# Two of the probability chunks of a tile turned by DMA instead of by TensorE

## What is computed

```
xn = layernorm(x)
scores = (xn @ W_qk) @ xn^T / 16 + (kpos - qpos) * slope, causal
s = softmax(scores) @ (xn @ W_v^T)
g = silu(top-1 mixture of 8 experts (256 -> 1024 -> 256) of xn, 512 tokens for each expert at most)
out = x + s * g
```

## Time and profile before

| | us |
|---|---|
| median of 3 runs | 500.19 (499.97 to 501.13) |
| profiled execution | 500.93 |
| its span | 499.2 |
| PE busy | 443.4 (89%) |
| DVE busy | 352.4 (71%) |
| ACT busy | 258.1 (52%) |
| POOL busy | 229.4 (46%) |

### The profile page before, as it was taken

One profiled execution on the slowest core, in us unless ns is written; L12 is line 12 of the kernel. 1 busy time (PEld: TensorE's weight loads), 2 busy tenths in 40 slices (PEclk: granted clock), 3 DMA queues, 4 the chain that ended last, 5 costly groups with the idle time before them and its releaser, 6 DMA issues.

```text
span 499.2 us, 8775 instructions
## 1 busy us (share of the span) xinstructions
PE 443.4 (89%) x3137; PEld 303.3 (61%) x3137; DVE 352.4 (71%) x949; ACT 258.1 (52%) x540; POOL 229.4 (46%) x339
## 2 busy tenths in 40 slices
PE   2778498989999898998999999999999999999970
PEld 1345265666677775675776678666666666666650
DVE  2869478688676777787776564597888979787440
ACT  1443334445455533453533445686776868677640
POOL 4218641460514072645013000328787687878761
PEclk9979789999999998999999999999999999999995
DMA  8961430430710186406001504408577574752140
GB/s 265 372 258 44 129 127 19 128 120 6 208 44 0 23 282 189 145 2 191 21 1 37 130 13 169 128 9 247 177 204 222 158 234 116 244 128 74 62 126 31
DMA packets 64315, 63.45 MB, mean 127 GB/s; under 512 B 36902, under 2 KB 58156, under 8 KB 62224
## 3 DMA queue, kind: packets, MB, share of 16 engines
q1 hardware_dynamic: 53472, 40.78, 27.9%
q0 software_dynamic: 5632, 16.73, 10.5%
q10 hardware_dynamic: 5168, 5.37, 3.3%
HBM read 30.29 MB, written 25.43 MB: 112 GB/s over the span
## 4 chain that ended last, share of the span: by engine, by line
PE 36%; DVE 32%; ACT 11%; issue 5%; POOL 5%; SPq 1%; DMA 1%; POOLq 0%; DVEq 0%; ACTq 0%
PE bank L1101 11%; PE bank L1103 11%; PE bank L1102 11%; DVE pmax L825 7%; DVE w_l L851 6%; DVE hid_l L869 4%; PE bank L1172 4%; ACT sc L1004 4%; DVE sc L794 3%; DVE pT_l L807 2%; POOL xn L518 2%; ACT hid_h L1027 2%; ACT hid L1025 1%; ACT w_h L1016 1%; POOL slots L572 1%
## 5 line engine op out<-in xcount | busy, mean ns | idle before, releaser
L1010 ACT ACTIVATE pT_h<-bank 128x512 f16<-128x512 f32 (+2 forms) x80 | 42.0, 528 | 75.2 <-PE bank L1172 75.1
L807 DVE TENSOR_TENSOR pT_l<-bank,pT_h 128x512 f16<-128x512 f32 (+2 forms) x80 | 48.5, 607 | 37.1 <-ACT pT_h L1010 37.1
L1101 PE MATMUL bank<-v_h,pT_h 128*128 128x256 f16 x272 | 74.2, 273 | 0.4 <-DVE pT_l L807 0.4
L1102 PE MATMUL bank<-v_l,pT_h 128*128 128x256 f16 x272 | 74.2, 273 | 0.0
L1103 PE MATMUL bank<-v_h,pT_l 128*128 128x256 f16 x272 | 74.2, 273 | 0.0
L1004 ACT ACTIVATE sc<-sc,nbias 128x512 f32<-128x512 f32 (+2 forms) x80 | 51.8, 649 | 43.1 <-DVE nbias L800 43.1
L1101 PE MATMUL bank<-w_h,hid_h 128*128 128x256 f16 x256 | 69.9, 273 | 2.9 <-DVE w_l L851 2.8
L869 DVE TENSOR_TENSOR hid_l<-hid,hid_h 128x512 f16<-128x512 f32 x64 | 50.1, 789 | 29.7 <-ACT hid_h L1027 29.6
L1102 PE MATMUL bank<-w_l,hid_h 128*128 128x256 f16 x256 | 69.8, 273 | 0.0
L1103 PE MATMUL bank<-w_h,hid_l 128*128 128x256 f16 x256 | 69.8, 273 | 0.0
L1101 PE MATMUL bank<-xT,qT_h 128*128 128x512 f16 (+3 forms) x160 | 56.1, 354 | 8.2 <-DVE cmax L794 5.7
(11 more groups left out here) (164 smaller groups left out, 986.4 us busy)
## 6 DMA issues: line engine op xcount, KB each, us to landing
raw<-in_w_e SPq DMA_DIRECT2D x5, 2048.0 KB, 8.8
sc<-in_w_e SPq DMA_DIRECT2D x3, 2048.0 KB, 7.6
slots<-empty ACTq DMA_DIRECT2D x1, 4224.0 KB, 28.9
out<-xg SPq DMA_DIRECT2D x8, 512.0 KB, 3.3
rows<-xg SPq DMA_DIRECT2D x8, 512.0 KB, 4.4
rows<-so SPq DMA_DIRECT2D x8, 512.0 KB, 3.0
xg<-in_x SPq DMA_DIRECT2D x6, 512.0 KB, 4.3
xg<-in_x ACTq DMA_DIRECT2D x2, 512.0 KB, 6.0
```

What stands on the lines that cost most here:

```text
L807: v.tensor_tensor(pT_l[:, t % 2, cols], tr_ps[n % 2][:, 0:w], pT_h[:, t % 2, cols], ALU.subtract).then_inc(pT_lo, 1)
L1010: a_.activation(pT_h[:, t % 2, c * GTOK:c * GTOK + w], tr_ps[n % 2][:, 0:w], ACT.Copy).then_inc(pT_hi, 1)
L1101: pe.matmul(ps, a_h, b_h, start=first, stop=False, skip_group_check=shared)
L1102: pe.matmul(ps, a_h, b_l, start=False, stop=False, skip_group_check=shared)
```

## The change

In tiles with three or four chunks, chunks 0 and 2 no longer go through PE's turn. ACT copies the probabilities to f16 directly behind their exponential, in query layout, into a slot of `hid_h`; DVE makes the low half into `hid_l` at the head of step 0 or 1 (`low_early`), ahead of the score it reads there; and SP issues two DMA transposes for the chunk (`turn_p`), into `pT_h` and `pT_l`. Both chunks of tile t stand in SP's list ahead of what it had for tile t. PE's `values` wait for the two landings. The other chunks keep their way, with the two banks counted by `turn_no`.

```diff
+def by_dma(t, c):
+    return chunks(t) >= 3 and c % 2 == 0
+def dma_no(t, c):
+    return sum(by_dma(k, q) for k in range(t) for q in range(chunks(k))) + sum(by_dma(t, q) for q in range(c))
+def turn_no(t, c):
+    return chunk_no(t, c) - dma_no(t, c)
...
 SP
+            def turn_p(t, c):
+                d, w = dma_no(t, c), chunk_blocks(t, c) * P
+                cols = slice(c * GTOK, c * GTOK + w)
+                sp.wait_ge(p_lo, d + 1)
+                sp.wait_ge(pv_full, t - 1)
+                for half, turned_half in ((hid_h, pT_h), (hid_l, pT_l)):
+                    sp.dma_start_transpose(turned_half[:, t % 2, cols].rearrange("p (q n) -> p q n", n=P),
+                                           half[:, d % HB, 0:w]).then_inc(pT_in[d % HB], 16)
...
             for t in range(TILES):
                 g = t // GT
+                for c in range(chunks(t)):
+                    if by_dma(t, c):
+                        turn_p(t, c)
                 if t % GT == 0 and g + 1 < GROUPS:
                     group_out(g + 1)
...
-            sp.wait_ge(turned, ALL_CHUNKS)
+            sp.wait_ge(turned, ALL_CHUNKS - DMA_CHUNKS)
+            sp.wait_ge(p_lo, DMA_CHUNKS)
 DVE
+            def low_early(t, c):
+                d, w = dma_no(t, c), chunk_blocks(t, c) * P
+                dve.wait_ge(p_hi, d + 1)
+                v.tensor_tensor(hid_l[:, d % HB, 0:w], sc[:, t % 2, c * GTOK:c * GTOK + w], hid_h[:, d % HB, 0:w],
+                                ALU.subtract).then_inc(p_lo, 1)
...
                 for c in steps(t):
+                    if c < 2 and c * 2 < chunks(t) and by_dma(t, c * 2):
+                        low_early(t, c * 2)
                     if c < chunks(t + 1):
                         score(t + 1, c)
-                    if c < chunks(t):
+                    if c < chunks(t) and not by_dma(t, c):
                         low(t, c)
 ACT, in probs
                     a_.activation(sc[:, k, cols], sc[:, k, cols], ACT.Exp, bias=nbias[:, k:k + 1],
                                   accum_out=psums[:, t % 3, c:c + 1]).then_inc(exp_made, 1)
+                    if by_dma(t, c):
+                        d, w = dma_no(t, c), chunk_blocks(t, c) * P
+                        act.wait_ge(exp_made, chunk_no(t, c) + 1)
+                        if d >= HB:
+                            act.wait_ge(pT_in[d % HB], d // HB * 32)
+                        a_.activation(hid_h[:, d % HB, 0:w], sc[:, k, cols], ACT.Copy).then_inc(p_hi, 1)
...
-                    if c < chunks(t):
+                    if c < chunks(t) and not by_dma(t, c):
                         high(t, c)
 PE
             def values(t, c):
-                n, at = chunk_no(t, c), key_slot(t // NT, c)
-                pe.wait_ge(pT_lo, n + 1)
+                at = key_slot(t // NT, c)
+                if by_dma(t, c):
+                    d = dma_no(t, c)
+                    pe.wait_ge(pT_in[d % HB], d // HB * 32 + 32)
+                else:
+                    pe.wait_ge(pT_lo, turn_no(t, c) + 1)
...
-                    if c < chunks(t):
+                    if c < chunks(t) and not by_dma(t, c):
                         turn(t, c)
```

More of the change, by code:

```diff
@@ L89 @@
 ALL_CHUNKS = sum(chunks(t) for t in range(TILES))
+DMA_CHUNKS = dma_no(TILES, 0)
 def layer_kernel(nc, x, w_qk, w_v, slope, w_r, w_e, out, slots, rows, tops):
@@ L277, in layer_kernel @@
         pT_lo = sem("pT_lo")
+        p_hi = sem("p_hi")
+        p_lo = sem("p_lo")
+        pT_in = [sem(f"pT_in{k}") for k in range(HB)]
         pv_full = sem("pv_full")
@@ L801, in score @@
                                     ).then_inc(nbias_made, 1)
+            def low_early(t, c):
[3 more added lines that the diff above has]
+                                ALU.subtract).then_inc(p_lo, 1)
             def low(t, c):
-                n, w = chunk_no(t, c), chunk_blocks(t, c) * P
+                n, w = turn_no(t, c), chunk_blocks(t, c) * P
                 cols = slice(c * GTOK, c * GTOK + w)
@@ L1164, in turn @@
             def turn(t, c):
-                n = chunk_no(t, c)
-                pe.wait_ge(exp_made, n + 1)
+                n = turn_no(t, c)
+                pe.wait_ge(exp_made, chunk_no(t, c) + 1)
                 if n >= 2:
```

## The result

The changed kernel takes 509.65 us in the median of 5 runs (508.26 to 510.90) against 499.97 (498.96 to 501.13, 5 runs) on the same chip: a ratio of 1.0192, 95% interval 1.0168 to 1.0216. It is slower, by 9.7 us. The forecast was 507.4, in a range of 495 to 520. The profiled execution took 508.26 with a span of 506.2, the one before 500.93 with 499.2, so the two traces explain 7.0 to 7.3 us. The rest is spread between executions: the profiled one is the fastest of the five after the change, 1.4 us under their median, and the one before lies 1.0 over its median.

A forecast was written before the change was run, and what follows sets the result against it. The prediction took PE's order of work as the bound. 14.7 us saved on PE against queue stalls, ACT and DVE delays and 4.4 us of slow clock left the end 7.2 us late: 507.4 us, range 495 to 520.

The forecast's parts named there:

- the four places: Chunk 0 of tiles 8, 11, 15 and 30, where PE would wait 2, 5, 7 and 4 us for a DMA.
- the sum: All terms added along PE's path: 13.3 us late at tile 15, 4.1 before tile 30, 7.2 at the end.
- What is removed: On PE: 116 blocks at 0.109 us, 12.6 us, and three waits for a first exponential; together 14.7 us.
- The transposes: 64 on SP's queue: a chunk's two halves need 4.3 us, hidden in an undisturbed tile.
- ACT and DVE: Tiles 8 to 15: new copies and subtractions delay score reads, 1.5 us in tile 10, and eat what tiles 12 to 14 save.
- The queue: SP works its list in order, so chunk 0 comes 1.7, 7.6, 11.6 us late at tiles 8, 11, 15, 2.3 more at 30.
- The clock: PE at half speed behind the waits at tiles 11, 15 and 30: 1, 1.7 and 1.7 us, 4.4 in all.
- Everything lands in time: Rival: no chunk is late at any tile, so 14.7 us off, 485.5 us; chance 0.09.
- DVE absorbs its part: Rival: only the queue's stalls cost, DVE's idle time takes its new work, 497.5 to 499 us; chance 0.19.
- The transposes were not slow: Answers the rival that transposes land after 8.0 us, chunk 0 2 us late in each of 16 tiles, 540 us; chance 0.11.

The follow-up runs named there:

- r_seq2x: Changed kernel with chunks 0 and 2 by DMA in the second sequence alone, without chunk 0 of tile 30; 494.37 us, ratio 0.9881 to the kernel before.
- r_seq2o: Changed kernel with the DMA chunks in the second sequence alone, (30, 0) included, and SP's list around tile 30 reordered; 493.29 us, ratio 0.9851 to before.
- r_skip: Changed kernel with (8, 0), (11, 0), (15, 0), (15, 2) and (30, 0) left to TensorE; 498.20 us, ratio 0.9955 to the kernel before.
- v_place: Changed kernel with five chunks left to TensorE, ACT's copy behind the exponentials and DVE's low half behind the score read; 495.51 us, ratio 0.9899 to before.
- q_order: Changed kernel with only SP's list reordered around tiles 8, 11, 15 and 28 to 30; 505.44 us, ratio 1.0119 to the kernel before.
- q_place: Changed kernel with ACT's copy moved behind the exponentials and DVE's low half behind the score read; 508.42 us, ratio 1.0179 to the kernel before.
- q_warm: Changed kernel with 34 useless matmuls before the wait of values(15, 0) and 20 before that of values(30, 0); 504.27 us, ratio 1.0107 to before.
- v_best: Changed kernel with (8, 0), (11, 0), (15, 0), (15, 2) on PE, first sequence's copies and low halves placed behind, SP's list reordered at tile 30; 491.74 us, ratio 0.9817.
- q_two: Changed kernel with chunk 2 alone by DMA, chunk 0 by PE as before; 499.95 us, ratio 0.9997 to the kernel before.
- t_after: Changed kernel with the weights' pieces of tiles 8 to 15 cut from 512 to 16 columns; 510.46 us, against 498.90 for the kernel before with the same cut.

## Why the prediction was right, step by step

The sign, the four places and the sum held (7.2 us forecast at the end, 7.0 measured between the traces, 9.7 between the medians). Late, in us, at each step, forecast and measured (PE or N(t) after minus before):

| step | forecast | measured |
|---|---|---|
| values(8, 0) | 1.7, waiting 2 | 2.3, waiting 2.94 |
| N(11) | 3 | 2.0 |
| values(11, 0) | 7.6, waiting 5 | 5.9, waiting 2.20 |
| N(15) | 6.5 | 3.6 |
| values(15, 0) | 11.6, waiting 7 | 9.1, waiting 8.11 |
| behind tile 18 | 9.1 | 8.4 at N(19), 7.5 at N(20) to N(24) |
| saved from N(24) to N(29) | 5.0 | 5.7 |
| N(29) | 4.1 | 1.8 |
| values(30, 0) | 6.4, waiting 4 | 5.8, waiting 4.96 |
| end | 7.2 | 7.0 |

That the sum is off by 0.2 us only is luck. At N(15) it had charged 2.9 too much and at N(29) still 2.3; tile 30, where N(29) to values(30, 0) was to add 2.3 and added 4.0, put 1.7 of that back, and the way from there to the end 0.4. At tile 30 the two next_rows held the queue for 7.1 us (287.53 to 294.63) where the forecast took 6.2, the round trip of the top took 3.97 for 3.65, and the pair 4.8 for 4.26.

- *What is removed.* Right: PE's busy time fell by 10.0, with two stretches of half clock in it for the one of before, and r_seq2x and r_seq2o, where nothing new is late, gained from N(24) to N(31) the 6.4 and 6.8 that 46 and 50 blocks and two waits make at 0.109 us a block. The rows of the two waits were put down to tiles 27 and 28; they are in 28 and 29.
- *The transposes.* Right: 1.20 and 1.27 us of queue, landing in the median after 2.5, so a chunk needs 3.8 to 4.8 us at the four places (4.26 forecast), and no other chunk is waited for. The figure of the Trainium skill that spoke against the change ("VectorE: DVE Perf Modes", The three transpose paths, 1309 ns for a block by DMA), taken block by block, is not borne out for this shape: four blocks held the queue for 1.27 us and landed after 2.5.
- *ACT and DVE.* Right in tile 10, over the whole too dear: N(11) 2.0 and N(15) 3.6 late in place of 3 and 6.5. The low half takes 0.68 us in the attention (the experts' row that I took gives 0.79). At tile 11 the term that was mis-sized is the wait: 2.75 us of what I put on the DMA were a wait for the row maximum, at 128.69, just in front of it. That this place cost is no chance: r_skip takes back 9.3 us without any stall of the queue, v_place 3.0. And the stalls at tiles 8 and 11 did not add to it, as the sum had them: with the queue freed N(15) is 3.3 late (q_order), with the place changed 2.7 (q_place), with both 2.4 early (v_place, which leaves the two chunk 0s to PE), against 3.6 in the changed kernel. Up to N(15) either cost alone makes nearly the whole delay.
- *The queue.* Right as the cause of the waits at tiles 8, 11 and 30 (q_order). At tile 15 it is only one of two causes: the low half was ready at 177.9, 7.6 after N(15), because two copies, the split of group 5 and the weights' half stand in front of it on ACT (forecast: N + 2.5 in an undisturbed tile, and SP alone set the end). With turn(5) holding the queue until 180.76 the chunk went out at 180.86 either way, so the sum did not feel this, by luck; q_order did.
- *The clock.* Charged 4.4 us for three stretches. There are two, behind the waits of 8.11 and 4.96; none at tile 11, whose wait was 2.20. q_warm puts them at 1.7 and 2.2 us. The 4.2 us that the sum gave back at tile 18 (the wait of 2.47 and 1.7 of slow stretch) were 3.3 (N(18) 10.8 late, N(20) 7.5); the slow stretch there is worth the 0.9 that r_seq2x shows at N(20). The Trainium skill, "TensorE: Matmul & The Clock Gate", Loop structure matters more than you think (a long wait for a DMA, then matmuls at the lower clock), has 0.50 behind both on its side; behind the wait of 2.94 us for a DMA at tile 8 the clock stayed at 1.00.
- *The rivals.* "Everything lands in time" failed on SP's order, which is what it was said to decide on, and on the place of the new work too (r_skip). With both put right v_best gained 8.7 us by the medians of the 14.7. "DVE absorbs its part" is refuted by r_skip and q_two. The transposes were not slow in the changed kernel: only the chunks at the four places were waited for.
- Mine missed in the experiments: q_order was to bring 490 and brought 505.4, for I had put the whole of tiles 9 to 15 down to the queue; and q_two 495.5 for 499.95.

Open: 1.3 of r_skip's 9.3 us, how the length of the weights' pieces and the new work share the loss of tiles 9 to 14, the slow landing in t_after, and what decides whether the clock falls behind a wait.

## What to carry to other kernels

Before work is moved from a full engine to a DMA, list what its queue does in order, and find the items that wait for something themselves (a round trip, another engine's half): each of them is a wall for whatever is queued behind it. The replacement work counts by where it stands and not only by how long it takes: up to N(15) the same copies and subtractions took 6.3 us more in front of the reads that free the full engine's banks than behind them. When one of two such costs is removed and the time stays, the other is standing behind it; remove both in one kernel before either is judged (here that turned 1.9% of loss into 1.8% of gain, with four chunks of the first sequence left to TensorE). And before a gain of 1 us is read from two traces, compare them at a point that the edit does not reach.

## What the runs showed of the hardware

- A DMA transpose of 128x512 f16 holds its queue for 1.20 to 1.27 us (medians; single ones up to 2.42) and lands after 2.5 us in the median, but the last half took 2.9, 2.6, 3.2 and 3.6 us at the four places, and the slowest of each trace 4.4 (after) and 4.6 (t_after).
- PE's clock fell to 0.50 behind waits of 8.11 and 4.96 us, to 0.57 behind one of 2.18 (r_skip and q_order), and did not behind waits of 2.20, 2.75 and 2.94 in the changed kernel and 2.97 in q_two (at 194.40). Behind the same wait at tile 18 it fell in one trace (2.47, before) and not in another (2.49, r_seq2x). The length of the wait alone does not tell it, and the same instructions can run either way.
- 34 matmuls of 128x512 in front of the wait at tile 15 kept the clock at 1.00 behind it and ended before the landing, so they delayed nothing there.
